# Causal attention core: the shift of a hyperbolic head is issued with the scores of the head before it, and ring waits name the engine that frees the bank

## The reference, cut to what matters

```
outs.append(_sdpa(q[:, :N1], k[:, :N1], v[:, :N1], 1.0 / math.sqrt(HD)))
outs.append(_hyp_attn(q[:, N1:N1 + N2], k[:, N1:N1 + N2], v[:, N1:N1 + N2], curvature))
outs.append(_sdpa(qn, kn, v[:, N1 + N2:], math.sqrt(HD)))

def _hyp_attn(q, k, v, curv):
    tq = jnp.sqrt(1.0 / curv + jnp.sum(q * q, axis=-1, keepdims=True))
    tk = jnp.sqrt(1.0 / curv + jnp.sum(k * k, axis=-1, keepdims=True))
    inner = jnp.einsum('bhtd,bhsd->bhts', q, k) - tq * jnp.swapaxes(tk, -1, -2)
    arg = jnp.maximum(-curv * inner, 1.0 + 1e-07)
    dis = jnp.sqrt(1.0 / curv) * jnp.arccosh(arg)
    scores = 1.0 / (eps + dis) + _causal_bias(q.shape[-2], k.shape[-2], q.dtype)
    return jnp.einsum('bhts,bhsd->bhtd', jax.nn.softmax(scores, axis=-1), v)
```

## Time and profile before

| | us |
|---|---|
| median of three runs | 5732.23 |
| lowest, highest | 5721.1, 5742.0 |
| profiled execution | 5748.39 |
| its span | 5746.7 |
| causal core in it, about | 1179 |

### The profile page before, as it was taken

The page is one execution under the profiler, slowest core; times in us unless marked ns, Lnnn a source line. Parts: engine busy times, 40 slices in busy tenths (PEclk is TensorE's granted clock), DMA queues, the critical chain, the costliest instruction groups (busy, mean ns, idle before and its releaser), DMA issues. The chain is left out here.

```text
span 5746.7 us, 99792 instructions
## 1 busy us (share of the span) xinstructions
PE 4422.5 (77%) x26575; PEld 2884.0 (50%) x26575; DVE 3816.5 (66%) x9299; ACT 2478.7 (43%) x5698; POOL 596.5 (10%) x928
## 2 busy tenths in 40 slices
PE   6999788300388885878787776776999998689898
PEld 5777566200255553555555555554555554344444
DVE  4555333588687877777767764555777777477776
ACT  2222333565333333677777762222666666200000
POOL 0111000000000001000000001111111111122221
PEclk9999899655699997777777787887999999899998
DMA  2222233679644443222222225555333333211110
GB/s 81 74 75 68 105 140 139 196 240 396 229 132 124 132 124 91 62 71 71 71 71 71 71 52 144 156 156 139 85 91 92 92 90 88 63 46 47 49 47 25
DMA packets 380380, 617.00 MB, mean 107 GB/s; under 512 B 43575, under 2 KB 310389, under 8 KB 380277
## 3 DMA queue, kind: packets, MB, share of 16 engines
q1 hardware_dynamic: 367956, 614.35, 36.6%
q0 software_dynamic: 12320, 1.40, 0.2%
HBM read 345.02 MB, written 269.21 MB: 107 GB/s over the span
## 5 line engine op out<-in xcount | busy, mean ns | idle before, releaser
L1670 DVE TENSOR_REDUCE e_neg<-ps 91x1 f32<-91x273 f32 x1536 | 571.8, 427 | 139.2 <-PE ps L1491 131.8
L1603 ACT ACTIVATE e_probT<-ps 91x273 f32<-91x273 f32 x1536 | 491.6, 392 | 291.7 <-PE ps L1491 290.9
L1218 PE MATMUL ps<-k_downT,f_o 128*91 128x256 f32 x1152 | 259.7, 385 | 455.9 <-DVE f_o L1126 455.7
L2345 PE MATMUL ps<-m_we,m_xT 128*128 128x512 f32 x1104 | 530.8, 630 | 0.0
L1218 PEld LDWEIGHTS ps<-k_downT,f_o 128*91 128x91 f32 x1152 | 182.8, 161 | 524.5 <-issue 456.9
L1489 PE MATMUL ps<-c_mask_kq,c_identb 91*91 91x91 bf16 x1536 | 322.7, 241 | 105.9 <-ACT g_probT L1603 74.3
L1491 PE MATMUL ps<-e_k,e_q 96*91 96x273 bf16 x1536 | 344.3, 306 | 62.9 <-DMA e_k<-s_parts 28.1
L2279 DVE SCALAR_TENSOR_TENSOR m_acc<-ps,m_weight,m_acc 128x256 f32<-128x256 f32 x552 | 261.7, 481 | 185.7 <-PE ps L2345 175.9
L1491 PE MATMUL ps<-g_q,g_k 102*91 102x273 bf16 (+5 forms) x1536 | 328.5, 294 | 50.6 <-DVEq L1676 49.9
L2345 PEld LDWEIGHTS ps<-m_we,m_xT 128*128 128x128 f32 x1104 | 214.8, 202 | 227.9 <-issue 213.5
L1491 PE MATMUL ps<-e_q,e_k 128*91 128x273 bf16 x1536 | 285.7, 290 | 40.1 <-DMA e_q<-e_shift 38.2
(11 more groups left out here) (306 smaller groups left out, 9733.9 us busy)
## 6 DMA issues: line engine op xcount, KB each, us to landing
s_gate<-b_gu SPq DMA_DIRECT2D x32, 819.0 KB, 4.7
s_up<-b_gu SPq DMA_DIRECT2D x32, 819.0 KB, 6.1
c_g<-s_gate SPq DMA_DIRECT2D x32, 819.0 KB, 7.2
s_gated<-c_g SPq DMA_DIRECT2D x32, 819.0 KB, 8.6
d_g<-s_gated SPq DMA_DIRECT2D x32, 819.0 KB, 10.4
d_u<-s_up SPq DMA_DIRECT2D x32, 819.0 KB, 10.7
s_o<-d_o SPq DMA_DIRECT2D x32, 819.0 KB
f_o<-s_o SPq DMA_DIRECT2D x32, 819.0 KB, 4.8
```

Of the source, the lines that this page charges most:

```text
L1218: last = nc.tensor.matmul(ps[0:R, t // 2, (t % 2) * D:(t % 2 + 1) * D], o[:, u, k, t * R:(t + 1) * R], downT[:, k, :], start=(k == 0), sto ...
L1603: nc.scalar.activation(probT[0:R, p % 8, b, :], src, ACT.Exp, scale=float(HD) ** 0.5 if kinds[h] == COS else 1.0)\
L1670: last = nc.vector.tensor_reduce(neg[:, u, t, h:h + 1], src, AX.X, ALU.max, negate=True)
L2345: last = nc.tensor.matmul(ps[0:R, EBANK[m % 4], :], xT[:, u, k, t * R:(t + 1) * R], we[:, k, 2 * p:2 * p + 2, :].rearrange("p e d -> p (e ...
```

## The change

PE issues a HYP head's two units of broadcast shift one main step earlier, right behind the scores of the head in front of it, and DVE adds them in that earlier step too. ACT's exponentials stay in the head's own step. For the causal core this gives the main steps 5: heads 11 and 8; 6: head 9; 7: none; 8: heads 4 and 6; 9: none; 10: heads 5 and 7; 11: none; all others as before. The order of the units round the ring does not change. The wait on `laid` moves with head 8 from step 6 to step 5. The wait for the ring's bank names who reads it: the addition (`shifted`) where the unit three before belongs to a HYP head, else the exponential.

```
+        issue = {p: [] for p in range(H)}
+        for p, h in enumerate(ORDER):
+            issue[p - 1 if h in HYPS else p].append(h)
+        issued = [h for p in range(H) for h in issue[p]]
...
@@ PE
-                if when == "main":
-                    h = ORDER[p]
+                for h in issue[p] if when == "main" else ():
                     if kinds[h] != COS:
                         x = [lo <= h < hi for _, lo, hi in shifts].index(True)
                         pe.wait_ge(laid[u], 16 * PARTS * (NSH * i + x + 1))
                     for b in range(UNITS):
-                        y = p * UNITS + b
-                        pe.wait_ge(S["exp"].sem, S["exp"].at(n, y - 2))
+                        y = issued.index(h) * UNITS + b
+                        before, unit = issued[max(y - 3, 0) // UNITS], (y - 3) % UNITS
+                        if y < 3:
+                            pe.wait_ge(S["exp"].sem, S["exp"].at(n, y - 2))
+                        elif before in HYPS:
+                            pe.wait_ge(S["shifted"].sem,
+                                       S["shifted"].at(n, hyp_slot[HYPS.index(before)] * UNITS + unit + 1))
+                        else:
+                            pe.wait_ge(S["exp"].sem, S["exp"].at(n, ORDER.index(before) * UNITS + unit + 1))
...
@@ DVE
-                if when == "main" and kinds[ORDER[p]] == HYP:
-                    a = HYPS.index(ORDER[p])
+                for h in [x for x in issue[p] if x in HYPS] if when == "main" else ():
+                    a = HYPS.index(h)
                     for b in range(UNITS):
-                        y = p * UNITS + b
+                        y = issued.index(h) * UNITS + b
                         dve.wait_ge(S["s"].sem, S["s"].at(n, y + 1))
```

## The result

| | before | changed |
|---|---|---|
| median, us | 5735.08 (4 runs, 5721.1 to 5742.0) | 5832.57 (4 runs, 5813.93 to 5835.78) |
| ratio | | 1.0166, 95% interval 1.0137 to 1.0196 |
| span of the profiled execution | 5746.7 | 5812.2 |

A forecast was written before the change was run, and what follows sets the result against it. A loop from DVE's looks 6 to 9 through ACT's scores and the shift to look 6 bounds the causal core: 34.08 - 0.70 + 5.17 = 38.55 us against 36.23, times 31 = +72, 5804 us; range 5750 to 5835.

The forecast's parts named there:

- (a): On PE, head 8 and its transfer wait move in front of look 6: a wait of 2.89 us a batch.
- the distance from send to look 6: From POOL's shift send to DVE's start on look 6: forecast 5.17 us, between 4.75 (high clock) and 5.58 (low).
- rest: The period from DVE's look 6 to POOL's next send: 34.08 us, read from one period, less 0.70 after the change.
- (b): DVE's two additions for head 8 move in front of look 6, hidden behind PE's work: gain 0.70 us a batch.
- (c): Heads 9, 6 and 7 also move a step forward on PE, their additions on DVE: taken as 0.
- (d): PE's ring waits name the addition instead of the exponential, and ACT's inputs are ready sooner: taken as 0.
- Shorter ring waits open the loop: Rival: PE's waits on ACT hold the chain between looks, naming the addition releases it; 5710 to 5641 us, chance 0.12.
- Slack behind: Rival: the delayed look 6 is made up before the next shift, no change, 5732 us; chance 0.08.
- Slower still: Rival: PE also falls behind at steps 8 and 10, clock low in every period; +100 us, 5832; chance 0.10.
- Signs: What the changed kernel's trace should show, among it POOL's sends 38.1 to 39 us apart, evenly.

The follow-up runs named there:

- e2: The changed kernel with only head 8 moved a step forward, heads 9, 6 and 7 in their own steps: sends 39.21 us apart, 1.0142 of before.
- e4: The changed kernel with head 8's broadcast reading k in place of q, so it needs no shift transfer: 36.34 us a period, 1.0011 of before.
- e1: The changed kernel with head 8 alone back at its own main step: 37.54 us a period, 1.0043 of before.
- e3: The kernel before with the ring waits by name and nothing moved: 36.31 us a period, 1.0005 of before.

## Why the prediction was right

The mechanism, its place and its sign came out as put; the size was too small by a quarter. The measured 5832.57 us lies above the band that I gave 0.70, 5791 to 5817 us, and only 2.4 us below the upper end of the range, 5835, so that the range held it with some luck.

- **(a), the wait of head 8.** The transfer's wait comes in all 32 batches, 2.1 us in the mean (1.3 to 4.0), the landing is 3.48 us after the send in the mean (3.40 forecast), and e2 and e4 show that this wait alone makes the loss. The step that was mis-sized is the distance from send to look 6. I took the middle of both clocks, 5.17 us; measured are 5.43. Of the 0.26 between them 0.09 is the later landing (3.49 in these 31 periods; 4.64 in one) and 0.17 PE's own work: in 19 of the 32 batches PE's first matmul after the landing lasts 0.30 or 0.31 us, as at 1.2 GHz, in the others 0.24. And I had worked from a single rest of 34.08 us, by which the mean distance of before would be 36.23 - 34.08 = 2.15 us; it was 1.95.
- **(b), the additions in idle time.** Forecast 0.70 us; the rest fell from 34.28 to 33.67, 0.61 us. The balance: (5.43 - 1.95) - 0.61 = 2.87 us against 2.32 forecast. The 0.55 between them is 0.26 from the new distance, 0.20 from the old one and 0.09 here. Times 31 it makes 17 us of the 29 by which the median lies above the forecast; 3 are the median of before, which a fourth run moved to 5735.08, and the others lie outside the periods.
- **(c), bunching.** Taken at 0, and e2 (39.21) beside the changed kernel (39.10) bears it out. In e1, where heads 8 and 9 stand in one step behind look 6, the rest is 0.83 us longer.
- **(d), ring waits.** Taken at 0, e3 gives 1.0005. The reason given was that ACT's wait of 4.35 us ended before another wait for DVE. e4 bears it out: ACT's waits for the added scores are down to 9.9 us, and the time is that of before.
- **Rivals.** "Shorter ring waits open the loop" needed the transfer hidden; e4 hides it and finds 1.0011, not faster. "Slack behind" fell: the 3.48 us came back one for one but for the 0.61. "Slower still" gave 5832, the very number, but its reason did not occur: nothing was lost in steps 8 and 10, DVE's dense stretch was as short as forecast, and only its clock half held in part.
- **Signs.** The sends lie 39.10 us apart in the mean, just outside the 38.1 to 39 named, and not evenly: single periods take 37.9 to 40.9 us.
- The Trainium skill ("TensorE: Matmul & The Clock Gate", section "What's actually happening") says that the array's clock falls when it idles; that every period would then take 5.58 us was my reading of it. The trace agrees in part: the granted clock of the core fell from 0.76 to 0.72 and the mean is 5.43 us, nearer to 5.58 than the middle I chose, but 13 of the 32 batches still begin head 8 at the high clock.

## What to carry to other kernels

Before an in-order engine's instruction is moved ahead, list what it waits for and what is now queued behind it: a wait that is harmless behind the work that feeds another engine can cost its whole length in front of it, as here. Find the loop that closes from batch to batch across engines and judge every edit by it; a shorter wait of an engine that next waits for the same producer was no gain here (ACT's 181.5 us down to 9.9 in e4, 1.0011). If such a loop exists, try to move its first instruction forward, not the ones that wait at its side (look 6 ahead, 0.9929), and expect a part of it to be lost in the rest (0.84 of 2.00 us there).

## What the runs showed of the hardware

Three shift transfers of 5.3 KB each are usable 3.3 to 3.6 us after the first send, in all 22 waits of before (3.29 to 3.44) and in 29 of the 32 of the changed kernel (2.84, 3.70 and 4.64 in the others), beside loads and stores of 65 to 70 GB/s. And PE is found at either of its two clock levels from period to period with nearly the same work: in the kernel before the distance from send to look 6 is 1.36 to 1.50 us in 21 periods, 3.38 to 3.53 in seven, in which PE's matmuls last as at 1.2 GHz, and between the two in three. That is 2.0 us beside an effect of 2.87, so that a mean over all periods is needed before two kernels are compared.
